# Graph layers on one Trainium2 core: segment sums by runs on VectorE in layer 0, edge weights turned on TensorE in layer 1

## The reference, cut to what matters

```python
h  = relu(LN(x))
x1 = x + segment_sum(h[src], dst) @ W_rel.T + b_rel + h @ W_root.T         # layer 0
h1 = relu(LN(x1))
w  = silu(edge_attr @ We1 + be1) @ We2 + be2                               # 200,000 x 128
out = x1 + h1 + silu(segment_sum(h1[src] * w, dst) @ Wn1 + bn1) @ Wn2 + bn2   # layer 1
```

## Time and profile before

| what | value |
|---|---|
| median of 3 runs (lowest, highest) | 4831.68 us (4816.43, 4837.42) |
| the profiled execution: its time, its span | 4849.66 us, 4847.9 us |
| busy share of the span: PE, PE's weight loads, DVE, ACT, POOL | 50%, 38%, 26%, 10%, 61% |
| mean granted TensorE clock | 0.665 |
| mean DMA rate | 61 GB/s |

### The profile page before, as it was taken

One profiled execution on the slowest core, in us unless ns is written; L12 is line 12 of the kernel. 1 busy time (PEld: TensorE's weight loads), 2 busy tenths in 40 slices (PEclk: granted clock), 3 DMA queues, 4 the chain that ended last, 5 costly groups with the idle time before them and its releaser, 6 DMA issues.

```text
span 4847.9 us, 35780 instructions
## 1 busy us (share of the span) xinstructions
PE 2418.4 (50%) x10938; PEld 1841.8 (38%) x10938; DVE 1276.0 (26%) x2181; ACT 479.4 (10%) x842; POOL 2970.8 (61%) x3135
## 2 busy tenths in 40 slices
PE   1332323232323232322447677777666777767667
PEld 0322322232222222222334445555454555544545
DVE  2511111111111111111323333333333333333334
ACT  3400000000000000000101111111111111111111
POOL 5366666666666666666465656666656666656662
PEclk9755556555656565655667767777767777767777
DMA  5222222222221222222222222222222222222222
GB/s 135 61 53 52 55 53 56 54 53 53 56 54 51 56 55 54 51 56 55 62 59 61 65 62 64 65 69 64 65 61 64 65 67 66 64 61 64 64 63 59
DMA packets 230579, 296.77 MB, mean 61 GB/s; under 512 B 68580, under 2 KB 160278, under 8 KB 230433
## 3 DMA queue, kind: packets, MB, share of 16 engines
q0 software_dynamic: 100096, 205.20, 16.8%
q10 hardware_dynamic: 61378, 60.59, 4.6%
q1 hardware_dynamic: 69086, 30.79, 2.4%
HBM read 269.87 MB, written 26.48 MB: 61 GB/s over the span
## 4 chain that ended last, share of the span: by engine, by line
another core or an unknown queue 44%; PE 26%; issue 17%; DVE 10%; DVEq 2%; ACT 1%; POOL 0%; DMA 0%; ACTq 0%; SPq 0%; POOLq 0%
PE seg_a L370 7%; PE seg_b L370 5%; PE ew_a L416 4%; PE ew_b L416 3%; DVE onehot L711 3%; PE hid_b L410 3%; PE hid_a L410 2%; DVE ew_a L817 2%; DVE rows L825 2%; DVE ew_b L817 1%; DVEq L719 1%; PE node L430 0%; DVE e_stats L625 0%; PE node L381 0%
## 5 line engine op out<-in xcount | busy, mean ns | idle before, releaser
L320 POOL DMA_INDIRECT rows<-h_rows,idx x3060 | 2905.5, 950 | 1783.2 <-issue 952.2
L370 PE MATMUL seg_a<-onehot,rows 128*128 128x128 f32 x3312 | 662.9, 358 | 1136.9 <-DVE onehot L711 445.2
L370 PEld LDWEIGHTS seg_a<-onehot,rows 128*128 128x128 f32 x3312 | 601.9, 268 | 1221.4 <-issue 934.2
L370 PE MATMUL seg_b<-onehot,rows 128*128 128x128 f32 x2944 | 572.5, 340 | 809.3 <-issue 576.9
L370 PEld LDWEIGHTS seg_b<-onehot,rows 128*128 128x128 f32 x2944 | 504.8, 249 | 855.7 <-issue 659.9
L711 DVE TENSOR_TENSOR onehot<-iota_ps,dst_rel 128x1536 f32<-128x1536 f32 (+1 forms) x278 | 461.3, 1659 | 1.0 <-DVE dst_rel L699 0.6
L817 DVE TENSOR_TENSOR ew_a<-ew_a,be_all 128x512 f32<-128x512 f32 x207 | 144.6, 699 | 1044.7 <-remote 703.2
L416 PE MATMUL ew_b<-we_sb,hidden 128*128 128x128 f32 x1472 | 289.3, 357 | 224.6 <-ACT hidden L578 177.1
L416 PEld LDWEIGHTS ew_b<-we_sb,hidden 128*128 128x128 f32 x1472 | 245.2, 252 | 406.5 <-ACT hidden L578 210.3
L416 PEld LDWEIGHTS ew_a<-we_sb,hidden 128*128 128x128 f32 x1664 | 268.6, 245 | 246.3 <-issue 169.0
L416 PE MATMUL ew_a<-we_sb,hidden 128*128 128x128 f32 x1664 | 310.8, 345 | 81.4 <-ACT hidden L578 55.2
(11 more groups left out here) (122 smaller groups left out, 1148.4 us busy)
## 6 DMA issues: line engine op xcount, KB each, us to landing
rows<-h_rows,idx POOLq DMA_INDIRECT x3060
ef_a<-ef_blocks ACTq DMA_DIRECT2D x70, 300.0 KB
node_work<-ef_blocks ACTq DMA_DIRECT2D x47, 300.0 KB
xs<-x SPq DMA_DIRECT2D x40, 256.0 KB
ys<-y_rows SPq DMA_DIRECT2D x26, 256.0 KB
out<-xs ACTq DMA_DIRECT2D x26, 256.0 KB
y_rows<-ys ACTq DMA_DIRECT2D x25, 256.0 KB
h_rows<-node_work ACTq DMA_DIRECT2D x23, 256.0 KB
```

Of the source, the lines that this page charges most:

```text
L320: pool.indirect_dma_start(out=rows[:, u, t, :], out_offset=None, in_=table, in_offset=bass.IndirectOffsetOnAxis(ap=idx[:, j:j + 1], axis=0 ...
L370: mm = pe.matmul(seg[g % 2][:, 0:P], rows[:, u, t, :], onehot[:, g % 2, k * TB + t, :], start=(k == 0 and t == 0), stop=(last and t == TB ...
```

## The change

Layer 0 no longer makes one-hots and multiplies per tile. The host reorders the edges within each group, so that partition p holds 12 neighbouring edges (8 in the last group) where it held every 128th. As `dst` is sorted, these 12 fall into few runs of equal target. At the start DVE numbers the runs of each partition and group by a scan. For each of R = 3 runs it then multiplies all 12 tiles with a mask (`picked`, 1536 columns over three PSUM banks, `wide`) and reduces over the tiles (`run_sum`, 128 columns); a one-hot of the three runs' targets (`run_hot`) and three matmuls on PE replace the twelve. Were there more than 3 runs in a partition, layer 0 would be done again in another turn; in the reference's inputs no partition of any group has more than 3. POOL waits for DVE's `s_sum` in layer 0, not for PE's `s_seg`.

```diff
+            def run_sums(i, it, g):          # on DVE
+
+                tiles = len(blocks_of(g)) * TB
+                first = g * GB
+                done = runs_summed(i, g) - RUN_STEPS
+                dve.wait_ge(s_sum, done)
+                v.tensor_tensor(run_mask[:, :, 0:tiles],
+                                dst_rel[:, bass.ds(it * U + first, tiles // TB), :].rearrange("p k t -> p (k t)")
+                                .unsqueeze(1).to_broadcast([P, R, tiles]),
+                                run_now.unsqueeze(2).to_broadcast([P, R, tiles]),
+                                ALU.is_equal).then_inc(s_mask, 1)
+                v.tensor_tensor(run_hot[g % 2], iota_ps.unsqueeze(1).to_broadcast([P, R, P]),
+                                run_dst[:, bass.ds(it * G + g, 1), :].rearrange("p g r -> p (g r)").unsqueeze(2)
+                                .to_broadcast([P, R, P]), ALU.is_equal)
+                dve.wait_ge(s_mask, i * G + (g + 1))
+                for r in range(R):
+                    if r > 0:
+                        dve.wait_ge(s_sum, done + 2 * r)
+                    v.tensor_tensor(picked[:, 0:tiles, :],
+                                    rows[:, first:first + tiles // TB, :, :].rearrange("p k t f -> p (k t) f"),
+                                    run_mask[:, r, 0:tiles].unsqueeze(2).to_broadcast([P, tiles, P]),
+                                    ALU.mult).then_inc(s_sum, 1)
+                    dve.wait_ge(s_sum, done + (2 * r + 1))
+                    v.tensor_reduce(run_sum[g % 2][:, r, :], picked[:, 0:tiles, :].rearrange("p e f -> p f e"),
+                                         AX.X, ALU.add).then_inc(s_sum, 1)
...
+            def run_sums(i, g):              # on PE
+                pe.wait_ge(s_sum, runs_summed(i, g))
+                for r in range(R):
+                    mm = pe.matmul(seg[0][g % 2][:, 0:P], run_sum[g % 2][:, r, :], run_hot[g % 2][:, r, :],
+                                   start=(r == 0), stop=(r == R - 1))
+                mm.then_inc(s_seg[0], 1)
...
-                    hold(pool, s_seg[layer], i * G + (g + 1))
+                    if layer == 0:
+                        hold(pool, s_sum, runs_summed(i, g) - RUN_STEPS * G)
+                    else:
+                        hold(pool, s_seg[1], i * G + (g + 1))
...
                     for g in range(G):
+                        dve.wait_ge(s_rows[0][g], landed(i, g))
+                        run_sums(i, it, g)
                         if g > 0:
                             add_window(0, i, it, g - 1)
...
-                        one_hot(it + (g + 1) // G, (g + 1) % G).then_inc(s_onehot, 1)
```

```diff
             def edge_weights(i, u):
                 pe.wait_ge(s_silu, i * U + (u + 1))
+                pe.matmul(hid_ps[u % 3][:, :], we2_sb[:, :], hidden[:, u % 2, :], start=True, stop=True
+                          ).then_inc(s_ew_t, 1)
+
+            def edge_turned(i, u):
+                pe.wait_ge(s_weights, i * U + (u + 2))
                 for t in range(TB):
-                    mm = pe.matmul(ew_ps[u % 2][:, t * D:(t + 1) * D], hidden[:, u % 2, t * P:(t + 1) * P],
-                                   we2_sb[:, :], start=True, stop=True)
-                mm.then_inc(s_ew, 1)
+                    tr = pe.transpose(ew_ps[u % 2][:, t * P:(t + 1) * P], weights[:, u % 2, t * P:(t + 1) * P],
+                                      ident[:, :])
+                tr.then_inc(s_ew, 1)
...
+            def edge_weights(i, u):
+                act.wait_ge(s_ew_t, i * U + (u + 1))
+                nc.scalar.activation(weights[:, u % 2, :], hid_ps[u % 3][:, :], ACT.Identity,
+                                     bias=be2_col[:, :]).then_inc(s_weights, 1)
...
+        seg = [[seg_ps, ew_ps[0]], [seg_ps, seg_ps]]
```

DVE's preparations (the zeroing of agg[0], the bases and the plan) are moved ahead of the loop that makes h, together with the new ones:

```diff
+            dve.wait_ge(s_dst, 16)
...
+            v.tensor_tensor_scan(run_of, scratch, run_of, 0.0, ALU.mult, ALU.add).then_inc(s_setup, 1)
...
+            def run_targets(n):
...
+                for r in range(R):
+                    out = run_dst[:, :, r].rearrange("p (i g) -> p i g", g=G)
+                    v.scalar_tensor_tensor(scratch, run_of, run_now[:, r:r + 1], dst_flat,
+                                           ALU.is_equal, ALU.mult).then_inc(s_pass, 1)
+                    dve.wait_ge(s_pass, n + (2 * r + 1))
+                    v.tensor_reduce(out[:, :, 0:G - 1], per_run[:, :, 0:full].rearrange(
+                        "p i (g e) -> p i g e", g=G - 1), AX.X, ALU.max)
...
+            run_targets(0)
             with dve.Fori(0, GROUPS // H_SETS) as k:
```

More of the change, by code:

```diff
@@ L274, in next_idx @@
                 load_idx(it + 1, HALF, U, s_idx_b)
[L276 removed]
+            with sp.Fori(0, passes0) as p:
                 next_idx(0, p * ITERS, 0)
@@ L351, in _ @@
             pe.wait_ge(s_ident, 1)
+            pe.wait_ge(s_run, 1)
+            pe.matmul(node[:, 0:P], scratch[:, 0:P], ident[:, :], start=True, stop=True).then_inc(s_run_max, 1)
             with pe.Fori(0, GROUPS // H_SETS) as k:
```

342 lines of the change are left out of this document (215 added, 127 removed).

## The result

| | kernel before | changed kernel |
|---|---|---|
| median of 4 runs (lowest, highest) | 4830.77 us (4816.43, 4837.42) | 5010.81 us (5006.84, 5014.38) |
| profiled execution: time, span | 4849.66, 4847.9 us | 5014.38, 5012.6 us |

The ratio is 1.0367, with a 95% interval of 1.034 to 1.0393: 180 us slower, where I had forecast 480 us, with 4640 to 5750 us as the range.

A forecast was written before the change was run, and what follows sets the result against it. POOL's gathers were taken as the bound, with signals 5 to 9 us late during long unbroken runs. Layer 0 +260, start +35, first looped iteration +50, between layers +20, layer 1 +115: +480 on 4831.7, about 5310 us; range 4640 to 5750.

The forecast's parts named there:

- the upper bound with doubled reductions: Layer 0: were DVE's strided PSUM reductions twice as long, DVE would bound it at about 100 to 125 us per iteration.
- six stops of 2.9 us are 17.4 us: Layer 0: POOL stops behind nearly every group as in layer 1, adding 17.4 us per iteration to 85 us of gathers.
- seven places at which DVE waits: Layer 0, each group: DVE waits for its own result or the rows, each wait 5 to 9 us beside gathers.
- The +50 for the first looped iteration: Layer 0's first looped iteration finds DVE still with the norms of the first rows, then its sums: +50 us.
- So I take +35 us for the restart: Start: 23 waits of DVE for its own results ahead of the h loop delay POOL's restart; bounds +10 and +120.
- The term of run_targets: Between the layers: run_targets called again, about 11 us, plus the last group's sums behind its rows, +9; together +20 us.
- The 12.30 us gather: Between the layers: DVE's 10.72 us zeroing held up one gather, read as agreeing with the DVE–GpSimd port lock; nothing charged.
- takes half of it there: Layer 1: PE's added weight matmul and transposes, +9 to +18 us per iteration, take half of PE's 29 us idle time.
- I take +5 us per iteration: Layer 1: the period grows 5 us in each of 23 iterations, +115 us in all; bounds 0 and +410.
- rival C: Layer 1 gains as much as layer 0 loses, DVE leaving the chain; within 0.5% of the old time; chance 0.05.
- signs that I had named for "wrong": Layer 0 iterations of 85 to 90 us without stops, reductions well above 1.7, restart before 180, layer 1 iterations under 102.
- A: Rival: without PE's small instructions POOL never stops in layer 0, 85.5 us per iteration, about 4690 us in all; chance 0.20.

The follow-up runs named there:

- seg_hold: Changed kernel, but in layer 0 POOL waits for PE's sum, as in the kernel before, instead of DVE's reductions; 4752.69 us, 56 us under the kernel before.
- prep_late: Changed kernel with DVE's preparations (runs, bases, plan, zeroing, targets) moved behind the loop that makes h; 5001.96 us.
- one_run_c: Changed kernel with one run per partition in place of three, measured in a session with late signals; 4698.65 us.
- after_again: The changed kernel itself, unchanged, in a session with prompt signals; 4048.19 us against 3998.98 for the kernel before, ratio 1.0122.

## Why the prediction was right or wrong

**The bound and the sign: right.** POOL is the bound, and the stops between its gathers come with late signals: with prompt signals there are none but the four of 2.6 to 2.9 us in the first looped iteration of layer 0. The forecast took it for granted that signals beside gathers are late; in a session of the other kind the same change costs 49 us. DVE's cost per operation was also right: 1.76 us for the product (forecast 1.75) and 1.756 for the reduction (1.71), 11.6 us per group (11.9), 69 us per iteration (71). The strided reduction out of PSUM costs what a contiguous pass does; the upper bound with doubled reductions has no case.

**Layer 0: +178 us instead of +310 (260 and 50).** The iteration came out near (106 us for 110), but by another way; that is luck. The step that failed is "I carry it over: six stops of 2.9 us are 17.4 us", with "seven places at which DVE waits", each priced at 5 to 9 us beside gathers. DVE's waits for itself at its products and reductions took 0.03 us beside the gathers. What comes late is PE's completion, and what becomes slow are register and wait instructions, which the 1.76 us operations mostly cover. So POOL runs on for 68 gathers and then stops once, for 7.6 us of lateness and 11.6 of DVE's group. I had asked how much work DVE has, and not what it stands in front of at the moment when POOL stops. seg_hold shows that this is the question: the same work, a later count, 10 to 11 us less per iteration. The +50 for the first looped iteration did not come; it lasted 94.8 us, 98.9 before. In a prompt session it is +10 (94.9 for 85.2).

**The start: -4 us instead of +35.** The step "So I take +35 us for the restart" priced 23 waits beside the gathers at up to 6.5 us. They took some 0.05 us each and 0.68 us at most, and the second pass of the loop behind them ended soon after POOL's gathers, with or without them (107 and 103 us). prep_late shows the cover: without it they cost 35 us. With prompt signals there is no such cover, and the start is 29 us later.

**Between the layers: +47 us instead of +20.** The term of run_targets was right (12.4 us for 11). The missed term is the backlog: I charged the last group's 9 us, but DVE, whose signals are late, hangs nearly a whole iteration behind POOL (15 of 18 reductions), and that remains when POOL is through. one_run_c bears this out (68.5 us between the layers, with a third of the work per group, where the changed kernel has 94.9), and so does after_again: there DVE has 4 reductions left and the term is +16 us, near my +20. The 12.30 us gather I had put down to the zeroing beside it; that reading was wrong, as the last section shows, though no term of the sum rests on it.

**Layer 1: -47 us instead of +115.** This is the largest error, and one of sign. The step was that PE, with 29 us idle, "takes half of it there", and so "I take +5 us per iteration". PE's busy time in the shown iteration is up by 5.4 us (78.08 for 72.65; 77.5 for 73.7 in the mean of the last 21 iterations), less than the 9 to 12 that I had, but POOL's stops do not follow PE's busy time. I had noted 29 us of PE's idle time and still charged half of its new work against the period. The gain itself I had only as half of rival C. Two of the signs that I had named for "wrong" came: POOL's restart before 180 us, and most iterations of layer 1 under 102 us.

**The rivals.** A (faster, 85.5 us per iteration) had its decisive point right for layer 0, that DVE's waits for itself stay at 0.1 us; but it left PE's completion out, on which DVE and so POOL still hang. In a prompt session its iterations are what happens, and even there the kernel is slower, by its edges. The Trainium skill ("SBUF — State Buffer", section "SBUF: two separate sides"), by which A would have been the case, speaks of SBUF's ports only; the 0.70 us instructions and the 1.1 us gathers of the late sessions come with bursts of gathers all the same. By which path is not shown. B (POOL and DVE taking turns) and its 136 us did not occur.

## What to carry to other kernels

When an engine stops for a count, look at what the producer is doing at that moment: if it stands for a signal with the counted work still ahead of it, the stop is lateness plus work, and it can be cheaper to wait for a later count whose work is already done. Work placed beside a stretch that is stretched by something else is free only as long as that stretch is; take its price from both ends. And after a long overlap, charge the whole backlog of the slower engine at its end, not its last step.

## What the runs showed of the hardware

- One and the same kernel takes 4000 or 4810 us, depending on the session. Where it takes 4810, register and wait instructions of SP (123 in its first trace), and with the changed layer 0 of DVE too, take 0.70 us or multiples of it late in long bursts of gathers, and PE's completions arrive up to 40 us late, 6 to 10 us after the gathers have stopped (1378.76 behind 1371.36 in the changed kernel, 1340.79 behind 1330.54 in seg_hold); where it takes 4000, there is not one such instruction. What this comes from is not known.
- In the late kind it also works the other way: in one_run_c 47 of the 69 gathers of the window shown took 1.0 to 1.8 us in place of 0.95, with POOL waiting for nobody. DVE's instructions of that stretch again come in steps of 0.7 us.
- Between the layers one gather again took 12.28 us (12.30 before), and it is not the zeroing alone that does it. At the start of the changed kernel the same zeroing (L721, 24.48 to 35.20 us) runs beside gathers of 0.94 us each. What does go with long gathers there are DVE operations that read two SBUF operands: one of 3.69 us beside the scan of 3.42 (L716), one of 2.21 beside a SCALAR_TENSOR_TENSOR of 1.85 (L739); a shorter one of 0.69 us (L924) left the gathers beside it at 0.95. Between the layers such an operation (L810, 1.53 us) stands right behind the zeroing, and the gather ends 0.8 us after it does. That the gather waits for that one is an inference; no run tests it. The products of layer 0, which read one operand from PSUM, leave the gathers beside them at 0.94 us.

```profile
24.48 10.72 DVE L721 MEMSET agg<- 128x12800 f32 x1 [2.61 <-issue]
...
2588.48 10.72 DVE L967 MEMSET agg<- 128x12800 f32 x1 [2.62 <-issue]
2599.12 1.53 DVE L810 TENSOR_TENSOR dst_rel<-dst_sb,sum_base 128x1380 f32<-128x1380 int32 x1
```
